# A recommendation tower on one core: weights in paced pieces, another chunk with the batch on the partitions, and gathers without a rest

## The chip, the cores and the metric

The kernel runs on one core of one Trainium2 chip. Times are device microseconds (us) of one execution. The figure that counts is the median of the runs.

## The reference

512 rows (the batch) look up one row of 64 numbers in each of 32 tables. For each of the 496 pairs of fields i < j, the reference takes p (field i) and q (field j), and a 64x64 matrix of that pair, and sums over both sides. The 496 sums of a batch row go through a small tower.

```python
e = jnp.stack([tbl_0[ids[:, 0]], ..., tbl_31[ids[:, 31]]], axis=1)      # 512 x 32 x 64
rows, cols = np.triu_indices(32, k=1)
p, q = e[:, rows, :], e[:, cols, :]
pij = jnp.einsum('bpe,dpe,bpd->bp', p, kernel, q)                        # 512 x 496
z = pij @ W.T + b                                                        # 512 x 256
h = jnp.concatenate([z, dense_ctx], axis=1)
h = jnp.maximum(h @ W_top1 + b_top1, 0.0)
h = jnp.maximum(h @ W_top2 + b_top2, 0.0)
y = h @ W_top3
```

## The kernel before, in words

**Chunks.** Two fields make a chunk, so there are 16 chunks of 128 numbers a batch row, and x_sb holds them with the batch of 512 along the free side. Chunks 0 to 3 (small tables) are picked by matmuls with one-hot matrices (pick_rows): VectorE makes three of four one-hots (L651), ScalarE the fourth. These picks fill the first 43 us. Chunks 4 to 15 are gathered from the tables by indirect DMAs on GpSimd (L339), 8 a chunk (2 fields by 4 tiles of 128 batch rows), 96 in all; gather k belongs to chunk 4 + k // 8. TensorE turns a gathered chunk (L393), and ScalarE copies it to x_sb and own_sb (L585, L589). This pair of steps is called "fill c" here: on TensorE it waits for all gathers up to number 8(c - 3) - 1 (fill 9: gather 47; fill 10: gather 55; fill 11: gather 63).

**Gathers.** A gather waits until the gather two before it has landed (FLIGHT = 2). Behind each gather stands a memset of 380 columns of a buffer that nobody reads (L346), the rest. GpSimd thus issues a gather, rests, and issues the next.

**Pair weights.** kern is loaded into k_sb in 16 slices of 8 blocks. Slices 0 and 1 come in 4 loads of 256 KB (L304), slice 0 right behind the tables of the one-hot fields, slice 1 once fill 0 is done. The other 14 slices come in 8 pieces of 64 KB each (L315), 112 pieces; piece p waits on the SP queue until gather 8 + p * 80 // 112 has landed. The upper half of k_sb is lent to the tables of the picks until fill 3 (L312).

**Units.** The work of TensorE is a fixed list. A group (g0 to g91) is the products of four field pairs with one chunk c (L439, L440; four of them, marked within, pair the fields of four chunks, L443 to L448), so it needs chunk c. VectorE multiplies its result with x_sb (L673), and later a reduce (L460, two for every four groups, called a reduce pair) sums over the 64 rows. A side unit (S0 to S31) does the same work for one quarter of the batch, for a chunk of FAR against the four chunks of NEAR (4 to 7), with the batch on the partitions: two matmuls (L414, L416), one multiply on VectorE with the gathered rows themselves (L660), and 16 sums on ScalarE (L570). A chunk of FAR has four side units, and thereby four groups fewer. t_ps has 3 buffers, so TensorE is at most three units ahead of VectorE; side_prod has 3, so VectorE is at most three side units ahead of ScalarE. There are 92 groups and 32 side units, with the blocks of k_sb in the order of the list.

**Order.** plan() puts fill c min(LEAD, (c - 1) // 2) groups before the first group that needs chunk c, and side unit m behind group SIDE_AT[m]. The order around the change is

```
fill 8 | g19 S2 g20 g21 R S3
fill 9 | g22 g23 g24 S4 g25 R g26 S5
fill 10| g27 g28 S6 g29 R g30 g31 S7
fill 11| g32 g33 R S8 g34 g35 S9 g36 g37 R S10 g38 g39
fill 12| ...
```

where R is a reduce pair. Each engine works through its own part of the list in order; ScalarE's copies for a fill stand behind the sums of the side units that come before that fill.

Of the kernel before, what the change touches and what calls it, by code (L numbers as in the profile page):

```python
# [13 lines left out]
P = 128  # L14
BATCH = 512
FIELDS = 32
EMB = 64
# [26 lines left out]


NEAR = [4, 5, 6, 7]
FAR = [0, 1, 8, 9, 10, 11, 12, 13]
SIDE_TILES = 8 * len(FAR)
SIDE_GROUPS = SIDE_TILES // 2
SIDE_UNITS = BT * len(FAR)  # L50


def is_side(c, a):
    return c in FAR and a in NEAR or c in NEAR and a in FAR


def side_tile(k, s, n):

    return 4 * (8 * (k % 2) + 4 * s + n) + k // 2
# [6 lines left out]
side_tiles = {side_tile(k, s, n): [(2 * c + s, 2 * near), (2 * c + s, 2 * near + 1)]  # L66
              for k, c in enumerate(FAR) for s in range(2) for n, near in enumerate(NEAR)}
GROUP = [(None, False, [side_tiles[2 * g], side_tiles[2 * g + 1]]) for g in range(SIDE_GROUPS)]
# [8 lines left out]
NT = 2 * len(GROUP)  # L77
WITHIN = [g for g in range(GROUPS) if MAIN[g][1]]
FIRST_GROUP = [min(g for g in range(GROUPS) if MAIN[g][0] == c) if c else 0 for c in range(CHUNKS)]
LEAD = 5  # L80

SIDE_AT = [15 + 71 * m // (SIDE_UNITS - 1) for m in range(SIDE_UNITS)]
SIDE = [(c, t) for c in FAR for t in range(BT)]


def plan():

    steps, chunks, side = [], 0, 0  # L90
    for g in range(GROUPS):
        while chunks < CHUNKS and (chunks < max(2, ONE_HOTS) or g >= FIRST_GROUP[chunks] - min(LEAD, (chunks - 1) // 2)):
            steps.append(("fill", chunks))
            chunks += 1
        steps.append(("group", g))
        while side < SIDE_UNITS and SIDE_AT[side] <= g:
            steps.append(("side", side))
# [13 lines left out]
for kind, n in UNITS:  # L111
    if kind == "side":
        c, t = SIDE[n]
        if t == 0:
            SIDE_BLOCK_OF[c] = len(BLOCK)
            BLOCK += [tuple((side_tile(FAR.index(c), s, k), (0, 1), 2 * c + s) for s in range(2)) for k in range(len(NEAR))]
        continue
    _, within, tiles = MAIN[n]
    g = SIDE_GROUPS + n
# [7 lines left out]
KS = 8  # L127
SLICES = BLOCKS // KS
# [13 lines left out]
ROWS_RING = 4  # L142
FLIGHT = 2
REST = 380
WARM = 2
PIECES = 8
PIECES_FROM, GATHERS_AHEAD = 2, 8
GATHERS = 2 * BT * (CHUNKS - ONE_HOTS)
HALF = BATCH // 2

# [10 lines left out]
def gathered_slot(n):  # L161

    return n if n < len(NEAR) else len(NEAR) + (n - len(NEAR)) % (G_RING - len(NEAR))


def build(nc, ids, ids_t, iota, pick, tables, kern, w_pairs, b_int, ctx_rows, w_ctx_rows, w1, b1, w2, b2, w3, ident, selector, out):
    steps = STEPS
    with ExitStack() as ctx:
        def sb(name, shape, dt=F32):
            return ctx.enter_context(nc.sbuf_tensor(name, shape, dt))  # L170

        def sem(name):
            return ctx.enter_context(nc.semaphore(name))
# [11 lines left out]
        k_sb = sb("k_sb", [P, BLOCKS, P])  # L185
# [28 lines left out]
        y_sb = sb("y_sb", [P, P])  # L214
        rest_sb = sb("rest_sb", [P, REST])
        zeros = sb("zeros", [P, BATCH])
# [31 lines left out]
        k_in = [sem(f"k_in{s}") for s in range(SLICES)]  # L248
# [7 lines left out]
        filled = sem("filled")  # L256
# [18 lines left out]
        rested = sem("rested")  # L275
# [11 lines left out]
        @block.sync  # L287
        def _(sp):
            sp.dma_start(ids_sb[:], ids.bitcast(U32).rearrange("(t p) f -> p t f", p=P)).then_inc(ids_in, 16)
            sp.dma_start(ident_sb[:], ident).then_inc(ident_in, 16)  # L290
            for f, field in enumerate(FIRST_FIELDS):
                if f == 4:
                    sp.wait_ge(one_hot_ready, OH_RING * 3 // 4)
                per = PICK[f][0]
                table = tables[field].rearrange("(p r) e -> p (r e)", r=per)
                for rows in (slice(0, DMA_ROWS), slice(DMA_ROWS, V_ROWS)):
                    sp.dma_start(table_sb[rows, f, 0:per].rearrange("p r e -> p (r e)"), table[rows]).then_inc(picks_in[f], 16)
            sp.dma_start(sel_sb[:], selector).then_inc(sel_in, 16)
            for s in range(PIECES_FROM):
                if s == 1:  # L300
                    sp.wait_ge(filled, 1)
                for half in range(2):
                    n = (2 * s + half) * KS * P
                    sp.dma_start(k_sb[half * EMB:(half + 1) * EMB, KS * s:KS * (s + 1), :].rearrange("p g m -> p (g m)"),  # L304
                                 kern[:, n:n + KS * P]).then_inc(k_in[s], 16)

            pieces = [(s, e) for s in range(PIECES_FROM, SLICES) for e in range(0, P, P // PIECES)]
            for p, (s, e) in enumerate(pieces):
                k = GATHERS_AHEAD + p * (GATHERS - 2 * GATHERS_AHEAD) // len(pieces)
                sp.wait_ge(rows_in[k % ROWS_RING], 16 * (k // ROWS_RING + 1))  # L310
                if s == SLICES // 2 and e == 0:
                    sp.wait_ge(filled, ONE_HOTS)  # L312
                half, low = e // EMB, e % EMB
                n = (2 * s + half) * KS * P
                sp.dma_start(k_sb[e:e + P // PIECES, KS * s:KS * (s + 1), :].rearrange("p g m -> p (g m)"),  # L315
                             kern[low:low + P // PIECES, n:n + KS * P]).then_inc(k_in[s], 16)
            for r in range(ROWS_RING):
                sp.wait_ge(rows_in[r], 16 * (GATHERS // ROWS_RING))
            for dst, src in LATE:
                sp.dma_start(dst, src).then_inc(late_in, 16)  # L320
            sp.wait_ge(y_kept, 1)
            sp.dma_start(out.rearrange("(t n) a -> t (n a)", t=BT), y_sb[::32, :]).then_inc(stored, 16)
            sp.wait_ge(stored, 16)

        @block.gpsimd
        def _(pool):
            pool.memset(w3_wide[:], 0.0).then_inc(w3_cleared, 1)
            pool.wait_ge(ids_in, 16)
            for n in range(CHUNKS - ONE_HOTS):
                if n >= G_RING:  # L330
                    pool.wait_ge(filled, n - (G_RING - len(NEAR)) + ONE_HOTS + 1)
                for f in range(2):
                    field = FIELD[2 * (n + ONE_HOTS) + f]
                    for t in range(BT):
                        k = (2 * n + f) * BT + t
                        landed = k - FLIGHT
                        if landed >= 0:
                            pool.wait_ge(rows_in[landed % ROWS_RING], 16 * (landed // ROWS_RING + 1))
                        pool.indirect_dma_start(  # L339
                            gathered[:, gathered_slot(n), t, f * EMB:(f + 1) * EMB], None, tables[field],  # L340
                            bass.IndirectOffsetOnAxis(ap=ids_sb[:, t, field:field + 1], axis=0),
                        ).then_inc(rows_in[k % ROWS_RING], 16)

                        if k:
                            pool.wait_ge(rested, k)
                        pool.memset(rest_sb[:], 0.0).then_inc(rested, 1)  # L346

        @block.tensor
        def _(pe):
            def warm_up():  # L350

                pe.wait_ge(zeros_ready, 1)
                for _ in range(WARM):
                    pe.matmul(sum_ps[:], zeros[:, 0:P], zeros[:], start=True, stop=True)
# [41 lines left out]
            def weights_in(k, blocks):  # L396

                for s in range(SLICES):
                    if k <= s * KS < k + blocks:
                        pe.wait_ge(k_in[s], 16 * (2 if s < PIECES_FROM else PIECES))  # L400

            def side_products(m):

                c, quarter = SIDE[m]
                u = UNITS.index(("side", m))
                k = SIDE_BLOCK_OF[c]
                if quarter == 0:
                    weights_in(k, len(NEAR))
                    pe.wait_ge(x_ready, 2 * (c + 1))
                pe.wait_ge(prod_ready, u - T_RING + 1)  # L410
                t = t_ps[:, u % T_RING]
                cols = slice(quarter * P, (quarter + 1) * P)
                low, high = slice(0, EMB), slice(EMB, P)
                pe.matmul(t[:, 0, :], x_sb[low, c, cols], k_sb[low, k:k + len(NEAR), :].rearrange("p g m -> p (g m)"),  # L414
                          start=True, stop=True)
                pe.matmul(t[:, 1, :], x_sb[high, c, cols], k_sb[high, k:k + len(NEAR), :].rearrange("p g m -> p (g m)"),  # L416
                          start=True, stop=True).then_inc(t_ready, 1)
# [329 lines left out]
```

## Time and profile before

| | us |
|---|---|
| median of 3 runs | 259.27 |
| lowest, highest | 256.65, 260.71 |
| the profiled execution, its time | 258.45 |
| its span | 256.6 |

The span is the stretch that the profile covers; 1.85 us of the execution's time lie around it. In the rows below, a PE row is TensorE's matmuls, PEld its weight loads, DVE VectorE, ACT ScalarE, POOL GpSimd, SPq the queue of SyncE. PE's busy time is modelled and holds short waits inside a run of matmuls; the idle times in brackets are the longer ones.

### The profile page before, as it was taken

The page shows a single profiled execution, that of the slowest core. Times are in us where ns is not written, and L with a number is a line of the kernel's source. Part 1 is how long each engine was busy: PE and PEld are TensorE (multiplying, and loading weights), DVE is VectorE, ACT ScalarE, POOL GpSimd, SP SyncE. Part 2 cuts the span into 40 slices and gives each one's busy share as a digit, 9 for nine tenths or more (in the row PEclk, how much of TensorE's full clock was granted, in tenths as well). Part 3 has the DMA queues.
Part 4 walks back from the last instruction along what each step waited for, and adds up shares of the span by engine and source line. Part 5 has one row for each costly group of instructions (what it writes and reads, how often), then busy time and mean ns, then how long its engine had stood idle before and what let it go on. Part 6 is the DMA issues. An engine that isn't in the chain of part 4 may idle for free.

```text
span 256.6 us, 4466 instructions
## 1 busy us (share of the span) xinstructions
PE 236.2 (92%) x1254; PEld 91.6 (36%) x1254; DVE 183.5 (72%) x205; ACT 174.1 (68%) x1110; POOL 136.9 (53%) x197
## 2 busy tenths in 40 slices
PE   7778789999999397949999999999999999999996
PEld 3433445233332132322243332333333233333474
DVE  2999995867778175845797878988888798860130
ACT  3867777032169908973989989998999969841121
POOL 5766988888888888888888878300000000000000
PEclk9799999999999779988999999999999999999999
DMA  6294232333333233333332321370000000000000
GB/s 163 67 278 117 69 82 61 75 85 88 76 82 82 74 89 77 74 82 76 84 83 72 83 70 25 78 251 3 1 1 3 1 0 3 1 0 0 3 0 0
DMA packets 11035, 16.43 MB, mean 64 GB/s; under 512 B 5166, under 2 KB 5810, under 8 KB 11010
## 3 DMA queue, kind: packets, MB, share of 16 engines
q1 hardware_dynamic: 7768, 12.97, 18.0%
q0 software_dynamic: 3072, 3.15, 6.6%
q8 instruction: 10, 0.16, 0.3%
q14 instruction: 15, 0.12, 0.2%
q10 hardware_dynamic: 170, 0.03, 0.1%
HBM read 16.13 MB, written 0.00 MB: 63 GB/s over the span
## 4 chain that ended last, share of the span: by engine, by line
PE 55%; POOL 26%; DMA 14%; issue 4%; ACT 0%
PE t_ps L439 22%; POOL gathered L339 18%; DMA gathered<-in_tbl,ids_sb 13%; PE sum_ps L460 12%; PE t_ps L414 9%; POOL rest_sb L346 8%; PE t_ps L505 3%; PE tp_ps L467 1%; PE t_ps L514 1%; PE t_ps L467 1%; PE tp_ps L393 1%; PE t_ps L443 1%; DMA ids_sb<-in_ids 1%; PE t_ps L447 1%; PE tp_ps L514 1%
## 5 line engine op out<-in xcount | busy, mean ns | idle before, releaser
L570 ACT ACTIVATE side_prod<-side_prod 128x64 f32<-128x64 f32 x512 | 122.6, 241 | 25.6 <-DVE side_prod L660 21.4
L673 DVE TENSOR_TENSOR prod<-t_ps,x_sb 128x1024 f32<-128x1024 f32 x88 | 104.2, 1216 | 30.2 <-PE t_ps L440 25.7
L339 POOL DMA_INDIRECT gathered<-in_tbl,ids_sb x96 | 94.7, 986 | 25.4 <-issue 13.6
L570 ACT ACTIVATION_READ_ACCUMULATOR side_prod<-side_prod 128x1 f32 x512 | 95.9, 187 | 0.0
L439 PE MATMUL t_ps<-x_sb,k_sb 64*128 64x512 f32 x176 | 92.1, 635 | 0.2
L440 PE MATMUL t_ps<-x_sb,k_sb 64*128 64x512 f32 x176 | 92.2, 635 | 0.0
L439 PEld LDWEIGHTS t_ps<-x_sb,k_sb 64*128 64x128 f32 x176 | 31.0, 193 | 47.5 <-issue 30.8
L460 PE MATMUL sum_ps<-prod,sel_sb 128*32 128x512 f32 x368 | 44.3, 598 | 0.0
L660 DVE TENSOR_TENSOR side_prod<-t_ps,gathered 128x1024 f32<-128x1024 f32 x32 | 38.9, 1216 | 7.1 <-PE t_ps L416 5.4
L346 POOL MEMSET rest_sb<- 128x380 f32 x96 | 42.1, 438 | 0.1
L416 PE MATMUL t_ps<-k_sb,x_sb 64*128 64x512 f32 x64 | 33.9, 610 | 0.0
L414 PE MATMUL t_ps<-k_sb,x_sb 64*128 64x512 f32 x64 | 33.9, 610 | 0.0
L440 PEld LDWEIGHTS t_ps<-x_sb,k_sb 64*128 64x128 f32 x176 | 31.0, 193 | 0.0
L651 DVE TENSOR_SCALAR pair_sums<-ids_bc,iota_sb 125x512 bf16<-125x512 f16 x57 | 24.3, 488 | 1.7 <-issue 1.2
L460 PEld LDWEIGHTS sum_ps<-prod,sel_sb 128*32 128x32 f32 x368 | 9.6, 109 | 31.9 <-issue 25.4
L585 ACT COPY x_sb<-tp_ps 128x512 f32<-128x512 f32 x14 | 8.1, 578 | 18.2 <-issue 11.3
L381 PE MATMUL tp_ps<-pair_sums,k_sb 125*64 125x512 bf16 x72 | 15.9, 410 | 4.5 <-DVE pair_sums L651 1.7
L414 PEld LDWEIGHTS t_ps<-k_sb,x_sb 64*128 64x128 f32 x64 | 10.9, 186 | 19.8 <-issue 11.1
L393 PE MATMUL tp_ps<-ident_sb,gathered 128*128 128x128 f32 x48 | 8.3, 299 | 10.2 <-DMA gathered<-in_tbl,ids_sb 9.7
L381 PE MATMUL sum_ps<-pair_sums,k_sb 125*64 125x512 bf16 x76 | 14.6, 382 | 1.7 <-DVE pair_sums L651 1.0
L553 ACT ACTIVATE distance<-ids_bc,iota_sb 125x512 f16<-125x512 f16 x17 | 12.1, 713 | 1.8 <-PE tp_ps L381 1.6
L393 PEld LDWEIGHTS tp_ps<-ident_sb,gathered 128*128 128x128 f32 x48 | 5.3, 147 | 19.6 <-issue 18.5
(66 smaller groups left out, 171.3 us busy)
## 6 DMA issues: line engine op xcount, KB each, us to landing
k_sb<-in_kern SPq DMA_DIRECT2D x112, 64.0 KB
gathered<-in_tbl,ids_sb POOLq DMA_INDIRECT x96
k_sb<-in_tbl SPq DMA_DIRECT2D x5, 280.0 KB
k_sb<-in_kern SPq DMA_DIRECT2D x4, 256.0 KB
w_sb<-in_w SPq DMA_DIRECT2D x2, 512.0 KB, 5.2
k_sb<-in_tbl SPq DMA_DIRECT2D x3, 224.0 KB
w_pairs_sb<-in_w_pairs SPq DMA_DIRECT2D x1, 512.0 KB, 3.6
ctx_sb<-in_ctx_rows SPq DMA_DIRECT2D x1, 192.0 KB, 6.0
```

The source lines that it names most:

```text
L339: pool.indirect_dma_start(gathered[:, gathered_slot(n), t, f * EMB:(f + 1) * EMB], None, tables[field], bass.IndirectOffsetOnAxis(ap=ids_s ...
L346: pool.memset(rest_sb[:], 0.0).then_inc(rested, 1)
L381: mm = pe.matmul(bank[half:half + EMB, :], part[:, f, r, :], one_hot[:, n % OH_RING, :], start=(r == 0 and part is high_sb), stop=(r == PI ...
L414: pe.matmul(t[:, 0, :], x_sb[low, c, cols], k_sb[low, k:k + len(NEAR), :].rearrange("p g m -> p (g m)"), start=True, stop=True)
L416: pe.matmul(t[:, 1, :], x_sb[high, c, cols], k_sb[high, k:k + len(NEAR), :].rearrange("p g m -> p (g m)"), start=True, stop=True).then_inc ...
L439: pe.matmul(t[:, 0, :], k_sb[low, k, :], x_sb[low, a, :], start=True, stop=True)
L440: pe.matmul(t[:, 1, :], k_sb[high, k, :], x_sb[high, a, :], start=True, stop=True).then_inc(t_ready, 1)
L460: mm = pe.matmul(sum_ps[32 * j:32 * j + 32, :], sel_sb[:, 30 - 2 * k:62 - 2 * k], prod[:, (t // 2) % PROD_RING, t % 2, :], start=(k == 0), ...
L570: one = act.activation(part, part, ACT.Copy, accum_out=side_sums[:, t, 16 * k + n:16 * k + n + 1])
L651: dve.tensor_scalar(one_hot[:, n % OH_RING, :], ids_bc[:, f, :], iota_sb[:, PICK[f][1] + r:PICK[f][1] + r + 1], None, ALU.is_equal).then_i ...
L660: dve.tensor_tensor(side_prod[:, g % SIDE_RING].rearrange("p s (c n) -> p s c n", c=len(NEAR)), t_ps[:, u % T_RING].rearrange("p s (c n) - ...
L673: dve.tensor_tensor(prod[:, g % PROD_RING], t_ps[:, u % T_RING], q, ALU.mult).then_inc(prod_ready, 1)
```

## The change

The pair weights of all 16 slices come in paced pieces (128 of them; piece p waits for gather 8 + p * 80 // 128, so slice s is asked for by gather 5s + 12 at the latest). The 4 loads of 256 KB and their wait are gone. FAR has chunk 14 in place of chunk 8. Chunk 8 thereby has 8 groups and no side units, chunk 14 has 10 groups and 4 side units; the totals stay. LEAD is 4 in place of 5, and SIDE_AT ends at 85 in place of 86. The first 16 gathers have no rest.

```diff
-FAR = [0, 1, 8, 9, 10, 11, 12, 13]
+FAR = [0, 1, 9, 10, 11, 12, 13, 14]
-LEAD = 5
+LEAD = 4
-SIDE_AT = [15 + 71 * m // (SIDE_UNITS - 1) for m in range(SIDE_UNITS)]
+SIDE_AT = [15 + 70 * m // (SIDE_UNITS - 1) for m in range(SIDE_UNITS)]
+NO_REST = 16
-PIECES_FROM, GATHERS_AHEAD = 2, 8
+GATHERS_AHEAD = 8
-            for s in range(PIECES_FROM):
-                if s == 1:
-                    sp.wait_ge(filled, 1)
-                for half in range(2):
-                    n = (2 * s + half) * KS * P
-                    sp.dma_start(k_sb[half * EMB:(half + 1) * EMB, KS * s:KS * (s + 1), :].rearrange("p g m -> p (g m)"),
-                                 kern[:, n:n + KS * P]).then_inc(k_in[s], 16)
-
-            pieces = [(s, e) for s in range(PIECES_FROM, SLICES) for e in range(0, P, P // PIECES)]
+            pieces = [(s, e) for s in range(SLICES) for e in range(0, P, P // PIECES)]
-                        if k:
-                            pool.wait_ge(rested, k)
-                        pool.memset(rest_sb[:], 0.0).then_inc(rested, 1)
+                        if k >= NO_REST:
+                            if k > NO_REST:
+                                pool.wait_ge(rested, k - NO_REST)
+                            pool.memset(rest_sb[:], 0.0).then_inc(rested, 1)
-                        pe.wait_ge(k_in[s], 16 * (2 if s < PIECES_FROM else PIECES))
+                        pe.wait_ge(k_in[s], 16 * PIECES)
```

The list after the change, from the same place on:

```
fill 8 | g19 S2 g20 g21 R S3 g22 g23 g24 S4 g25 R
fill 9 | g26 S5 g27 g28 S6 g29 R g30 S7
fill 10| g31 g32 g33 R S8 g34 g35 S9 g36
fill 11| g37 R S10 g38 g39 S11 g40 g41 R g42 S12 g43 g44 S13
fill 12| ...
```

Here g22 to g29 need chunk 8, g30 to g34 chunk 9, g35 to g40 chunk 10, g41 on chunk 11. The order up to fill 8 is unchanged.

## Rows read from the trace of the kernel before

**Rows 1.** The page, part 1: busy us (share of the span) and instructions of each engine.

```profile
PE 236.2 (92%) x1254; PEld 91.6 (36%) x1254; DVE 183.5 (72%) x205; ACT 174.1 (68%) x1110; POOL 136.9 (53%) x197
```

**Rows 2.** Waits, longest first: engine, line, awaited, us in total, times, longest.

```profile
PE tp_ps L393 <- DMA gathered<-in_tbl,ids_sb: 9.7, 3, 4.5
...
POOL gathered L339 <- DMA gathered<-in_tbl,ids_sb: 9.6, 15, 1.7
```

**Rows 3.** Timeline of PE around the three waits: start us, us, line, count, idle before.

```profile
82.63 0.59 PE L414 MATMUL t_ps<-k_sb,x_sb 64*128 64x512 f32 x1
...
87.76 1.09 PE L393 MATMUL tp_ps<-ident_sb,gathered 128*128 128x128 f32 x4 [4.53 <-DMA gathered<-in_tbl,ids_sb]
...
101.16 0.63 PE L393 MATMUL tp_ps<-ident_sb,gathered 128*128 128x128 f32 x4 [1.82 <-DMA gathered<-in_tbl,ids_sb]
```

**Rows 4.** Busy by stretch: PE, PEld, DVE, ACT, POOL, then granted clock, DMA share, GB/s.

```profile
83.20:87.80 4.60, 0.07 (x3) 0.07 (x2) 1.22 (x1) 4.60 (x41) 4.10 (x7) 0.86 0.33 83
87.80:93.20 5.40, 5.40 (x14) 2.51 (x16) 1.81 (x2) 2.52 (x15) 4.74 (x8) 0.50 0.31 76
...
99.30:101.20 1.90, 0.08 (x3) 0.07 (x2) 1.58 (x2) 1.20 (x11) 1.45 (x3) 1.00 0.23 56
101.20:110.00 8.80, 8.80 (x48) 3.30 (x48) 6.23 (x6) 8.29 (x63) 7.84 (x12) 1.00 0.35 85
110.00:113.40 3.40, 0.06 (x3) 0.04 (x1) 1.87 (x2) 1.84 (x17) 2.93 (x6) 1.00 0.31 72
113.40:117.50 4.10, 4.10 (x12) 1.56 (x12) 1.23 (x1) 3.48 (x23) 3.60 (x6) 0.58 0.32 76
```

**Rows 5.** The chain that ended last, in order of time: start us, us, what.

```profile
12.62 5.77 DMA gathered<-in_tbl,ids_sb
18.64 4.69 DMA gathered<-in_tbl,ids_sb
...
97.99 3.04 DMA gathered<-in_tbl,ids_sb
...
110.59 2.56 DMA gathered<-in_tbl,ids_sb
113.39 0.73 PE tp_ps L393 x4
...
117.58 1.85 PE sum_ps L460 x16
119.43 0.62 PE t_ps L414
120.06 0.42 PE t_ps L414
...
227.15 0.59 PE tp_ps L423 x4
```

**Rows 6.** Timeline of PE: the end of group g36.

```profile
123.48 0.59 PE L439 MATMUL t_ps<-x_sb,k_sb 64*128 64x512 f32 x1
```

**Rows 7.** Timeline of POOL: gathers 9, 10, 16, 47, and a rest between.

```profile
23.59 0.95 POOL L339 DMA_INDIRECT gathered<-in_tbl,ids_sb  x1 [0.88 <-DMA gathered<-in_tbl,ids_sb]
24.54 0.52 POOL L346 MEMSET rest_sb<- 128x380 f32 x1
25.23 1.07 POOL L339 DMA_INDIRECT gathered<-in_tbl,ids_sb  x1 [0.16 <-issue]
...
36.00 1.07 POOL L339 DMA_INDIRECT gathered<-in_tbl,ids_sb  x1 [0.16 <-issue]
...
85.14 0.95 POOL L339 DMA_INDIRECT gathered<-in_tbl,ids_sb  x1 [0.17 <-issue]
```

**Rows 8.** Busy by stretch, as rows 4, while tables and slices 0 and 1 load.

```profile
16.00:18.00 2.00, 0.87 (x8) 0.59 (x10) 2.00 (x6) 0.55 (x1) 0.92 (x2) 1.00 1.05 284
...
22.00:24.00 2.00, 1.76 (x12) 0.60 (x8) 1.97 (x4) 1.94 (x4) 1.12 (x3) 1.00 0.14 29
```

**Rows 9.** Timeline of SP: the four large loads and the first pieces.

```profile
14.90 4.26 SPq L304 DMA_DIRECT2D k_sb<-in_kern  x4
24.33 35.82 SPq L315 DMA_DIRECT2D k_sb<-in_kern  x31
```

**Rows 10.** Timeline of ACT: first and last of the 32 instructions of S3, then fill 9.

```profile
85.36 0.24 ACT L570 ACTIVATE side_prod<-side_prod 128x64 f32<-128x64 f32 x1
...
89.08 0.19 ACT L570 ACTIVATION_READ_ACCUMULATOR side_prod<-side_prod 128x1 f32 x1
89.17 0.57 ACT L585 COPY x_sb<-tp_ps 128x512 f32<-128x512 f32 x1
89.77 0.58 ACT L589 COPY own_sb<-tp_ps 64x512 f32<-64x512 f32 x1
```

## The prediction

> **What bounds the kernel now.** I read the page's busy shares first. TensorE is busy for 92% of the span, the others for at most 72% [rows 1]. A busy share does not say what stands in the other 8%, so the list of waits comes next: TensorE's longest wait for data is for gathers, 9.7 us in three waits of up to 4.5 us, in front of a turn [rows 2]. The timeline places them: fill 9 starts at 87.76 after 4.5 us idle, fill 10 at 101.16 after 1.8 us, fill 11 at 113.39 [rows 3, 5], where the gap is 3.3 us [rows 4]. The view by stretch shows what follows: behind the first wait the granted clock is 0.50 for 5.4 us and behind the third 0.58 for 4.1 us, which is TensorE's 1.2 GHz level; behind the 1.8 us wait it stays 1.00, 2.4 GHz [rows 4]. So three gathers (47, 55, 63) decide when TensorE goes on, and after fill 11 the chain that ended last stays on TensorE [rows 5]. From there on no gather is waited for. What is saved before fill 11 reaches the end; what is saved on gathers after it does not.
>
> **Part 1: chunk 14 for chunk 8, LEAD 4, SIDE_AT.** The number of products is the same. What moves is work that needs nothing newer than chunk 8: it now stands in front of fills 9, 10 and 11. The prices: a unit is two steps of 0.42 to 0.43 us, 0.86 us, a reduce pair takes 1.85 us, a turn at full clock about 0.6 us [rows 3, 5].
>
> TensorE reaches the wait of fill 9 at 83.2 now (its last side matmul starts at 82.63 and lasts 0.59) [rows 3]. After the change five units and a reduce pair stand there first: 83.2 + 5 x 0.86 + 1.85 + 0.2 for changes between kinds = 89.6. Gather 47 started at 85.14 [rows 7] and had landed by 87.6 (fill 9 started at 87.76). So no wait, and no slow clock.
>
> Fill 10 then comes after the turn, 8 units and a reduce pair: 89.6 + 0.6 + 6.9 + 1.85 = 99.0; with 0.6 for VectorE, which must keep up through three buffers, 99.6. Gather 55 landed at 97.99 + 3.04 = 101.0 [rows 5]. With gathers where they are, 1.4 us of wait are left and fill 10 starts at 101.2.
>
> Fill 11 comes again after a turn, 8 units and a reduce pair, 9.7 us: 110.9. Gather 63 landed at 110.59 + 2.56 = 113.15 [rows 5]: fill 11 starts at 113.4 as now, after 2.5 us idle, and ends at 114.0.
>
> What has been gained there: g0 to g36 and S0 to S9 are done. Before, that state (its fill 11 included) is reached at 123.48 + 0.5 = 124.0 [rows 6]. So 10.0 us, if gathers stay where they are and 2.5 us of idle do not lower the clock. Between 1.8 us (clock kept) and 3.3 us (clock lowered) the rows leave this open; if it falls, up to 1.7 us go back (four steps and a turn took 4.1 us at 0.58 in place of some 2.4) [rows 4]. The rest, from 124.0 to the end at 256.6, is 132.6 us of the same work.
>
> **Part 2: no rest for 16 gathers.** A rest takes 0.43 to 0.52 us, with 0.16 before the next gather; gathers 9 to 16 start 12.4 us apart in seven steps, 1.77 each (23.59 to 36.00) [rows 7]. Without it the limit is the landing of the gather two before. The undisturbed landing is 2.56 us after the start, and the next gather follows 0.26 us behind a landing (12.62 + 5.77 = 18.39 to 18.64) [rows 5], so the least step is (2.56 + 0.26)/2 = 1.41 us. Seven steps give back 7 x 0.36 = 2.5 us. Gathers 2 to 8 wait for landings already and gain little by this.
>
> **Part 3: no large loads.** Landings of 5.8 and 4.7 us are those of gathers 5 and 7, beside tables and slices 0 and 1; the DMA engines move 284 GB/s then, and 29 GB/s from 22 on [rows 5, 8]. The four loads, 1.0 MB, are issued from 14.90 on [rows 9]. At about 250 GB/s they hold the engines for 4 us. Without them gathers 6 to 9 come up to 4 us earlier; the lower bound is 0, if the tables alone delay them. I take 2.5, since the tables are queued first.
>
> The bill comes later. 128 pieces instead of 112 go beside the same 80 gathers, 1.6 each instead of 1.4. GpSimd waits for landings 15 times now, 9.6 us [rows 2]; the landing of gather 55, 3.04, is what two pieces close together cost. Up to gather 63 I take 1 us back, and another 1 us because gathers 16 on, now earlier, run beside the one-hots, where the gather instruction takes 1.07 instead of 0.95 us [rows 7]. Sum for gathers 47 to 63: 2.5 + 2.5 - 2 = 3 us earlier. Bounds: 1 us later (nothing gained, pieces cost) to 5 us earlier.
>
> The Trainium skill has a rule against this part. Its page "SBUF — State Buffer" (section "SBUF: two separate sides", with the box on the "DVE blocks DMA" trap) says that VectorE in a two-port mode, which tensor_scalar can take, shuts GpSimd out and starves it of descriptor writes. The trace agrees in sign, 1.07 beside 0.95 us, but not with a full block. By the rule the first 16 gathers gain nothing from the missing rest, which would leave rival A below.
>
> Are slices 0 and 1 in time? Slice 0 needs gather 12, slice 1 gather 17. Gather 16 starts at 36.00 now, so gather 12 has landed by 33 and slice 0 is in by 36; the first group runs at 43.7, and slice 1 is needed at about 53, in by 43. Covered even with no gain. The later slices are asked for up to 10 gathers later than now and needed tens of us after that.
>
> **Sum.** With gathers 3 us earlier, gather 55 lands at 98.0: no wait at fill 10 (99.6). Fill 11 is reached at 109.3, plus 0.4 for ScalarE's copy of chunk 10 (below): 109.7. Gather 63 lands at 110.2, fill 11 starts at 110.4 and ends at 111.0, at full clock. 111.0 + 132.6 = 243.6. Add 1.0 for ScalarE: **span 244.6, 12.0 us less**. The profiled time would be 258.45 - 12.0 = 246.4. The median shown is 0.8 above the profiled one: 259.27 - 12.0 = 247.3. I take **247.5**.
>
> **ScalarE.** The sums of a side unit take 3.8 us (85.36 to 89.17), a fill's copies 1.15 [rows 10]. Now ScalarE has gaps (busy 2.5 of the 5.4 us from 87.8) [rows 4]; after the change it has none: S3 ends at 89.2, S4 93.1, fill 9 94.3, S5 98.2, S6 102.1, S7 106.0, copies of fill 10 107.1. The first group of chunk 10, g35, would be reached at 106.7. So LEAD 4 costs 0.4 us there. Then come 24 side units (91.2), five fills (5.8) and three windows (0.6 each): 205.9. TensorE turns the side sums at 227.15 now [rows 5], 13 us earlier then, 214: ScalarE is done 8 us before. Counted the same way from fill to fill, its copies are 2 to 4 us ahead of the first groups. I take 1 us in all, at most 4.
>
> **Rivals.**
> A. Gathers come no earlier (the landing or the shared port holds them). Gain 10.0 - 1.0 for ScalarE, less up to 1.7 for the clock: 250.3 to 252.0, say 250.5. For it: gathers 2 to 8 wait for landings anyway, and the instruction is longer beside one-hots. Against it: gathers 10 to 16 wait for nothing but the rest [rows 7]. The page above would give this case.
> B. ScalarE becomes the bound: with LEAD 4 each of fills 10 to 15 waits about 1 us, and the rest costs 5 to 6 us instead of 1: gain about 7, 252.5. For it: it has no gap from 81 us on. Against it: the 8 us by which its sum stays short of TensorE's.
> C. Not faster: more pieces raise the landing. Before nothing is lost until the step exceeds a gather's own 1.55 us, that is a landing of 2.84. To eat the whole gain, gather 63 must land at 123.4, 10 us later: over 55 gathers 0.19 us a step, a mean landing of about 3.4 to 3.5 us. Such landings occur (3.04 for gather 55), but as exceptions. At a mean of 3.6, 262.
>
> **Chances.** Forecast (gathers 1.5 to 5 us earlier, 245 to 249) 0.53; even better, 244 to 245, 0.04; A (249 to 252) 0.25; B (252 to 255) 0.10; C (255 and more) 0.08. The range 244 to 252.5 holds 0.83 and leaves out C and most of B. A measurement of this kernel tells 2% from no change, 5.2 us: faster means below 254.1, chance 0.89; within 2% 0.08; slower 0.03.
>
> **What would show it.** Fill 9 starts without idle at about 89.6; fill 10 at 99.6; fill 11 by 110.4; granted clock 1.00 from 40 us on; gather 16 starts by 32, gather 47 by 82; GpSimd's waits for landings below 13 us in total; ScalarE busy without gaps from 81 us. Wrong: a new wait of TensorE for x_sb at the first group of a chunk (B), a step of the gathers above 1.8 (C), or first groups that wait for k_in.

## The result, and the profile after

| | before | after |
|---|---|---|
| median, us | 259.05 (4 runs) | 247.51 (4 runs) |
| lowest, highest | 256.65, 260.71 | 246.80, 248.09 |
| profiled execution, its time | 258.45 | 247.30 |
| its span | 256.6 | 245.5 |

The ratio is 0.9583, with a 95% interval of 0.9511 to 0.9656: 4.2% faster. This and all later ratios are of fast executions alone, where one that is more than 1.5% above the fastest of its kernel counts as slow. The code is some lines shorter, so L339 of before is L333 in the trace of after, L393 is L388, L439 L434, L460 L455, L585 L580, L589 L584. The kernels of the experiments have line numbers of their own, a few lines off.

The page of after, part 1 (busy us, share of the span, instructions), answers [rows 1]; the waits (us in total, times, longest) answer [rows 2]:

```profile
PE 232.3 (95%) x1254; PEld 89.8 (37%) x1254; DVE 177.0 (72%) x205; ACT 173.5 (71%) x1110; POOL 128.6 (52%) x181
```

```profile
POOL gathered L333 <- DMA gathered<-in_tbl,ids_sb: 16.5, 24, 2.1
...
PE tp_ps L388 <- DMA gathered<-in_tbl,ids_sb: 4.2, 3, 2.3
```

TensorE's waits for gathers fell from 9.7 to 4.2 us, 0.7 of it at fill 7. Its timeline (start us, us, line, idle before) at the first group and at fills 9, 10 and 11, against [rows 3, 5]:

```profile
40.49 0.69 PE L434 MATMUL t_ps<-x_sb,k_sb 64*128 64x512 f32 x1
...
87.03 0.66 PE L388 MATMUL tp_ps<-ident_sb,gathered 128*128 128x128 f32 x4
...
98.42 0.63 PE L388 MATMUL tp_ps<-ident_sb,gathered 128*128 128x128 f32 x4 [1.19 <-DMA gathered<-in_tbl,ids_sb]
...
110.66 0.63 PE L388 MATMUL tp_ps<-ident_sb,gathered 128*128 128x128 f32 x4 [2.34 <-DMA gathered<-in_tbl,ids_sb]
```

Fill 9 waits for nothing, as forecast. Fills 10 and 11 start at 98.42 and 110.66, where 99.6 and 110.4 were forecast, but both still wait. Two things in these rows were not forecast. The first group starts at 40.49 us instead of 43.71 (before: L439, first row of its kind), and the clock falls again behind fill 11. The view by stretch (columns as in [rows 4]):

```profile
108.30:110.70 2.40, 0.06 (x3) 0.07 (x2) 2.23 (x2) 2.40 (x22) 1.88 (x3) 1.00 0.41 103
110.70:115.70 5.00, 5.00 (x24) 1.25 (x24) 1.22 (x1) 4.15 (x28) 4.22 (x7) 0.66 0.34 80
```

The reduce pair behind fill 11 takes 3.1 us at this clock instead of 1.85. Gathers 16 and 63 on GpSimd, against [rows 5, 7] (36.00 and 110.59 there):

```profile
32.82 0.94 POOL L333 DMA_INDIRECT gathered<-in_tbl,ids_sb  x1 [0.30 <-issue]
...
108.09 0.95 POOL L333 DMA_INDIRECT gathered<-in_tbl,ids_sb  x1 [0.16 <-issue]
```

Gather 63 starts 2.5 us earlier; 3 us was forecast.

The experiments were to test these theories. G: only the time of the last gather waited for (63) and the work done before it decide. M: the rests on GpSimd hold up VectorE's one-hots. L, the rival of M: the large loads did. The executions of one kernel lie 1 to 5 us apart, a trace shows only one of them, and the intervals of the ratios are 1.1 to 1.7% wide. So small differences of the time show nothing unless the intervals are apart. Where a trace is compared with another, it is one execution against one.

### The profile page after: what moved, and what is told of

The parts are those of the page before. It is cut to its first block, busy times and chain, and to the rows that moved or that the text cites. A ratio compares the mean times of both kernels' runs of the same rounds, so it can differ in the third digit from the quotient of the medians.

```text
span 245.5 us, 4460 instructions
## 1 busy us (share of the span) xinstructions
PE 232.3 (95%) x1254; PEld 89.8 (37%) x1254; DVE 177.0 (72%) x205; ACT 173.5 (71%) x1110; POOL 128.6 (52%) x181
## 4 chain that ended last, share of the span: by engine, by line
PE 54%; DMA 22%; POOL 18%; issue 4%; ACT 0%
DMA gathered<-in_tbl,ids_sb 21%; PE t_ps L434 20%; POOL gathered L333 13%; PE sum_ps L455 12%; PE t_ps L409 8%; POOL rest_sb L341 5%; PE t_ps L500 3%; PE tp_ps L462 2%; PE t_ps L509 1%; PE t_ps L462 1%; PE tp_ps L388 1%; DMA ids_sb<-in_ids 1%; PE t_ps L438 1%; PE t_ps L442 1%; PE sum_ps L509 1%
## 5 line engine op out<-in xcount | busy, mean ns | idle before, releaser
L333 POOL DMA_INDIRECT gathered<-in_tbl,ids_sb x96 | 93.7, 976 | 32.5 <-DMA gathered<-in_tbl,ids_sb 16.5
L435 PE MATMUL t_ps<-x_sb,k_sb 64*128 64x512 f32 x176 | 88.7, 614 | 0.0
L434 PE MATMUL t_ps<-x_sb,k_sb 64*128 64x512 f32 x176 | 88.6, 613 | 0.1
L434 PEld LDWEIGHTS t_ps<-x_sb,k_sb 64*128 64x128 f32 x176 | 29.7, 185 | 45.2 <-issue 29.4
L455 PE MATMUL sum_ps<-prod,sel_sb 128*32 128x512 f32 x368 | 45.5, 613 | 0.0
L341 POOL MEMSET rest_sb<- 128x380 f32 x80 | 34.7, 433 | 0.0
L435 PEld LDWEIGHTS t_ps<-x_sb,k_sb 64*128 64x128 f32 x176 | 29.7, 185 | 0.0
L646 DVE TENSOR_SCALAR pair_sums<-ids_bc,iota_sb 125x512 bf16<-125x512 f16 x57 | 18.7, 385 | 4.2 <-ACT ids_bc L532 2.0
L455 PEld LDWEIGHTS sum_ps<-prod,sel_sb 128*32 128x32 f32 x368 | 9.8, 111 | 32.6 <-issue 28.0
L580 ACT COPY x_sb<-tp_ps 128x512 f32<-128x512 f32 x14 | 8.1, 581 | 16.4 <-PE tp_ps L388 11.0
L376 PE MATMUL tp_ps<-pair_sums,k_sb 125*64 125x512 bf16 x72 | 14.9, 410 | 3.1 <-DVE k_sb L625 1.7
L388 PE MATMUL tp_ps<-ident_sb,gathered 128*128 128x128 f32 x48 | 7.8, 284 | 4.5 <-DMA gathered<-in_tbl,ids_sb 4.2
L551 ACT ACTIVATE pair_sums<-distance 125x512 bf16<-125x512 f16 x17 | 10.7, 630 | 0.5
```

The costliest lines, as they stand in the source:

```text
L333: pool.indirect_dma_start(gathered[:, gathered_slot(n), t, f * EMB:(f + 1) * EMB], None, tables[field], bass.IndirectOffsetOnAxis(ap=ids_s ...
L376: mm = pe.matmul(bank[half:half + EMB, :], part[:, f, r, :], one_hot[:, n % OH_RING, :], start=(r == 0 and part is high_sb), stop=(r == PI ...
L434: pe.matmul(t[:, 0, :], k_sb[low, k, :], x_sb[low, a, :], start=True, stop=True)
L435: pe.matmul(t[:, 1, :], k_sb[high, k, :], x_sb[high, a, :], start=True, stop=True).then_inc(t_ready, 1)
L455: mm = pe.matmul(sum_ps[32 * j:32 * j + 32, :], sel_sb[:, 30 - 2 * k:62 - 2 * k], prod[:, (t // 2) % PROD_RING, t % 2, :], start=(k == 0), ...
L646: dve.tensor_scalar(one_hot[:, n % OH_RING, :], ids_bc[:, f, :], iota_sb[:, PICK[f][1] + r:PICK[f][1] + r + 1], None, ALU.is_equal).then_i ...
```

## The experiments

**One part alone: no rest behind 16 gathers** (e1_norest_alone), on the kernel before.

```diff
-                        if k:
-                            pool.wait_ge(rested, k)
-                        pool.memset(rest_sb[:], 0.0).then_inc(rested, 1)
+                        if k >= NO_REST:
+                            if k > NO_REST:
+                                pool.wait_ge(rested, k - NO_REST)
+                            pool.memset(rest_sb[:], 0.0).then_inc(rested, 1)
```

> The kernel before with one part: no rest behind the first 16 gathers. The trace after shows one-hots of VectorE at a mean of 385 ns against 488 before and the first group at 40.5 us against 43.7. If the rests on GpSimd hold the one-hots up (theory M), the one-hots have a mean near 385 to 400 here too, and the first group starts near 40.5. If it was the 1 MB of large loads beside them (theory L), it stays at 43.7. For the end, theory G (three gathers bound this order, the speed of the picks is worth nothing): only the shift of gathers 47 and 63 counts, 1 to 2.5 us, so 256.5 to 258 us. If the picks counted, the gain would be 3 us or more beside that of the gathers, under 254.

Ratio 0.9899 (0.9842 to 0.9956), 1.0%; the medians of all runs are 257.31 and 258.32. The groups of instructions of VectorE from 5 to 45 us (count, busy us, mean ns) in the kernel before and in this one, then the first group, gathers 16 and 63, and the turns of fills 9, 10 and 11:

```profile
L651 DVE TENSOR_SCALAR pair_sums<-ids_bc,iota_sb 125x512 bf16<-125x512 f16 x57 | 24.3, 488 | 1.7 <-issue 1.2 <-PE sum_ps L381 0.2
```

```profile
L653 DVE TENSOR_SCALAR pair_sums<-ids_bc,iota_sb 125x512 bf16<-125x512 f16 x57 | 19.4, 398 | 3.7 <-ACT ids_bc L539 1.8 <-PE sum_ps L383 1.1 <-PE tp_ps L383 0.5
```

```profile
41.10 0.69 PE L441 MATMUL t_ps<-x_sb,k_sb 64*128 64x512 f32 x1
```

```profile
33.28 0.94 POOL L340 DMA_INDIRECT gathered<-in_tbl,ids_sb  x1 [0.31 <-DMA gathered<-in_tbl,ids_sb]
...
107.56 0.95 POOL L340 DMA_INDIRECT gathered<-in_tbl,ids_sb  x1 [0.17 <-issue]
```

```profile
85.34 1.08 PE L395 MATMUL tp_ps<-ident_sb,gathered 128*128 128x128 f32 x4 [4.86 <-DMA gathered<-in_tbl,ids_sb]
...
98.13 0.63 PE L395 MATMUL tp_ps<-ident_sb,gathered 128*128 128x128 f32 x4 [1.95 <-DMA gathered<-in_tbl,ids_sb]
...
110.09 0.63 PE L395 MATMUL tp_ps<-ident_sb,gathered 128*128 128x128 f32 x4 [1.37 <-DMA gathered<-in_tbl,ids_sb]
```

Theory M holds: with this edit alone the one-hots take 398 ns and TensorE's groups start 2.6 us earlier. Gather 16 comes 2.7 us earlier, as the prediction worked out (2.5), and 63 comes 3.0 earlier. By the ratio the end gains 1.0%, about 2.6 us (its interval is 1.1 to 4.1 us), which fits the gathers' shift. The profiled execution gains more: it is the fastest of ten (253.37; two more lie below 254.5 and the rest at 256.7 to 258.3), and its span is 5.2 us shorter than that of before. Its trace shows from what. Fill 9 still waits 4.9 us, so the earlier picks are lost there. Fill 11 starts 3.3 us earlier, with the gathers. The other 1.9 us come from the clock. Here it fell behind fill 10 (0.70 from 98.1 to 102.0), and that delay only shortened the wait at fill 11; behind fill 11 it stayed at 1.00, where before it was 0.58 for 4.1 us. So theory G holds for the gathers, and the clock behind the last wait is a second term of about 2 us. Whether the same term explains the spread of the ten is not shown, since only one was profiled.

**One part alone: all weights in paced pieces** (e2_pieces_alone). The changed kernel with FAR, LEAD, SIDE_AT of before and NO_REST = 0.

> The kernel before with one part: all 16 slices of the weights in paced pieces, with rests behind all gathers. Theory L: the first group starts near 40.5 us, one-hots near 385 ns. Theory M: 43.7 and 488 as before. The landing of gathers 5 and 6 falls from 5.8 and 6.1 us to about 4, so gather 9 starts 2 to 3 us earlier; 128 pieces give 1 us back by gather 63. Theory G: 1 to 2 us faster than before, 257 to 258.5.

Ratio 0.9923 (0.9869 to 0.9976).

```profile
L646 DVE TENSOR_SCALAR pair_sums<-ids_bc,iota_sb 125x512 bf16<-125x512 f16 x57 | 23.9, 480 | 1.9 <-ACT ids_bc L532 1.4 <-PE sum_ps L376 0.2
```

```profile
22.13 1.06 POOL L333 DMA_INDIRECT gathered<-in_tbl,ids_sb  x1 [0.17 <-issue]
...
111.14 0.95 POOL L333 DMA_INDIRECT gathered<-in_tbl,ids_sb  x1 [0.17 <-issue]
```

Theory L falls: one-hots at 480 ns, first group at 43.69. Gather 9 (first row) starts at 22.13, 1.5 us earlier than before, but gather 63 at 111.14, 0.55 later. The profiled execution, 258.69 us, is at the upper end of this kernel's runs (254.2 to 259.1); the ratio says 0.8% faster, and this trace does not show from what.

**One part alone: the order** (e3_order_alone).

```diff
-FAR = [0, 1, 8, 9, 10, 11, 12, 13]
+FAR = [0, 1, 9, 10, 11, 12, 13, 14]
-LEAD = 5
+LEAD = 4
-SIDE_AT = [15 + 71 * m // (SIDE_UNITS - 1) for m in range(SIDE_UNITS)]
+SIDE_AT = [15 + 70 * m // (SIDE_UNITS - 1) for m in range(SIDE_UNITS)]
```

> The kernel before with one part: chunk 14 in place of chunk 8, LEAD 4, SIDE_AT 70. Theory G: the prediction's own sum with gathers where they are, 10.0 us less 1.0 for ScalarE and up to 1.7 for the clock: 249.5 to 252. Fill 9 without idle, fill 10 about 1.4 us, fill 11 about 2.5 us idle. A rival that gives the gathers most of the gain: under 4 us, above 255.

Median 249.77, ratio 0.9677 (0.9623 to 0.9730): 8.3 us. Fills 9, 10 and 11:

```profile
88.73 0.66 PE L393 MATMUL tp_ps<-ident_sb,gathered 128*128 128x128 f32 x4
...
100.90 0.63 PE L393 MATMUL tp_ps<-ident_sb,gathered 128*128 128x128 f32 x4 [1.96 <-DMA gathered<-in_tbl,ids_sb]
...
113.20 0.63 PE L393 MATMUL tp_ps<-ident_sb,gathered 128*128 128x128 f32 x4 [2.40 <-DMA gathered<-in_tbl,ids_sb]
```

Fill 9 without a wait, fills 10 and 11 within 0.3 us of the forecast 101.2 and 113.4. Behind the wait of 2.4 us the clock is 0.64 for 4.8 us. Against the kernel before, the ratios of e3 and of the full change are 0.9677 and 0.9583: by these ratios the order carries about three quarters of the gain (3.2 of 4.2%). Their intervals overlap, so the last quarter is not shown by the times.

**The rests put back** (e4_order_pieces): the changed kernel with NO_REST = 0.

> The changed kernel with the rests behind the first 16 gathers put back. Theory G: the end moves by what gather 63 loses, 1.5 to 2.5 us, so 249 to 250, and the slower picks (theory M: first group at 43.7 again) cost nothing beside that; fill 11 waits less than in the changed kernel (0 to 1 us instead of 2.3) and the clock stays up. If the picks counted: 3 us and more slower, above 250.5.

Median 249.97, ratio 0.9657 (0.9582 to 0.9732), beside e3's 0.9677: adding the pieces to the order changes nothing that can be measured. In its trace gather 16 starts at 35.46, gather 63 at 111.79 and fill 11 at 114.47 after 2.46 us idle. Gather 63 is 1.4 us later than in e3, with 16 pieces more. The expectation that fill 11 would wait at most 1 us was wrong: against the changed kernel the gathers lost as much (3.7 us) as TensorE's first group did (3.6). So this run cannot tell the cost of the gathers from that of the picks. Its profiled execution is also the slowest of its four, 251.08.

**The large loads put back** (e5_order_norest): order and missing rests, 4 loads of 256 KB and 112 pieces.

> The changed kernel with the 4 large loads of slices 0 and 1 back in place of 16 paced pieces (112 pieces over the same gathers). By the prediction the large loads delay gathers 6 to 9, so gather 63 would come 1.5 us later and the time be 248.5 to 249. By the runs of the single parts (gather 63 at 107.6 us with no rest alone and 112 pieces, at 108.1 in the changed kernel) the pieces give back by gather 63 what they gain by gather 9: gather 63 at 107.3 to 107.8, the time 246.5 to 247.5, the same within 0.3%.

Median 248.15 (247.4 to 248.5), ratio 0.9611 (0.9552 to 0.9671), not told apart from the changed kernel. Gather 63 at 108.97, 0.9 later than in the changed kernel; with e1 against the changed kernel it was 0.5 earlier and with e3 against e4 1.4 earlier. The pieces move gather 63 by no more than the scatter, to either side.

**LEAD 5** (e6_lead5).

```diff
-LEAD = 4
+LEAD = 5
```

> The changed kernel with LEAD 5 in place of 4, all else the same. The turns stand one group earlier in the list, so fill 11 is reached 0.9 us earlier and waits 0.9 us more for the same gather, with fewer groups done: 248 to 249, 1 to 1.5 us slower. If ScalarE's copies were late with LEAD 4 (rival B of the prediction), LEAD 5 would be faster instead: 245 to 246.5.

Ratio 0.9613 (0.9526 to 0.9700), median 248.76. Fill 10 waits 2.46 us, fill 11 3.33 (1.19 and 2.34 with LEAD 4), in an execution, the slowest of four, whose gather 63 was itself 2.2 us later. The direction is that of theory G; the ratio does not tell the two apart.

**No rest behind 64 gathers** (e7_norest64): NO_REST = 64.

> The changed kernel with no rest behind the first 64 gathers instead of 16. Theory G with steps at half the landing: landings of 2.6 to 3.1 us give steps of 1.43 to 1.68 against 1.62 now between gathers 16 and 47 and 1.56 up to 63; gather 63 starts 2 to 5 us earlier, fills 10 and 11 wait at most 1 us, the clock stays up: 243 to 245.5. Rival: the rest is what keeps the landings short; without it they grow to 3.1 and more, steps stay at 1.6 or rise, 247 to 249.

Median 248.86, ratio 0.9655 (0.9595 to 0.9715), not faster than the changed kernel. The profiled execution is the fastest of six, 245.57. Its waits:

```profile
POOL gathered L333 <- DMA gathered<-in_tbl,ids_sb: 35.1, 38, 1.9
```

Gather 16 at 32.43, gather 47 at 82.92: 1.63 us a step against 1.62 with rests, and gather 63 at 107.62. The rival holds: what GpSimd no longer rests it waits for landings, 35.1 us instead of 16.5. Beyond gather 16 the rest costs nothing.

**Two memsets as a rest** (e8_double_rest16): two memsets of 380 columns behind each of the first 16 gathers.

> The changed kernel with two memsets of 380 columns behind each of the first 16 gathers, where it has none and the kernel before one. Theory M, each memset holds up one-hots: mean of the one-hots 385 ns with none, 474 to 488 with one, 540 to 600 with two; first group at 45 to 47 us against 40.5 and 43.7. If instead any GpSimd instruction that is on slows them alike, gathers too, the mean stays under 500. The gathers themselves come later: gather 16 near 38 to 40, time 252 to 256.

One run of 252.7 us. One-hots at a mean of 497 ns, first group at 44.91, gather 16 at 38.99. The mean is below what was expected of theory M, since fewer gathers and so only 1.7 times as many memsets fall beside the picks; it lies even below the 500 that the expectation named as the sign of the other reading, that any GpSimd instruction slows the one-hots alike. The mean does not by itself tell memsets from other GpSimd work; the single one-hots and the run e11 below do. VectorE's timeline in the kernel before, four one-hots around the memset at 26.29 (0.47 us) that follows the gather at 25.23 [rows 7]:

```profile
25.39 0.34 DVE L651 TENSOR_SCALAR pair_sums<-ids_bc,iota_sb 125x512 bf16<-125x512 f16 x1
25.65 0.76 DVE L651 TENSOR_SCALAR pair_sums<-ids_bc,iota_sb 125x512 bf16<-125x512 f16 x1
26.33 0.58 DVE L651 TENSOR_SCALAR pair_sums<-ids_bc,iota_sb 125x512 bf16<-125x512 f16 x1
26.83 0.33 DVE L651 TENSOR_SCALAR pair_sums<-ids_bc,iota_sb 125x512 bf16<-125x512 f16 x1
```

A one-hot takes 0.34 us and starts 0.26 behind the one before. Two are longer. The one of 0.76 lies beside the end of the gather and the start of the memset, the one of 0.58 over the memset. Their followers start 0.68 and 0.50 behind them: 0.66 us lost for one gather and its rest. In the changed kernel, beside a gather without a rest (29.92 to 31.00), only one of the row is longer, and by 0.15:

```profile
30.36 0.35 DVE L646 TENSOR_SCALAR pair_sums<-ids_bc,iota_sb 125x512 bf16<-125x512 f16 x1
30.62 0.49 DVE L646 TENSOR_SCALAR pair_sums<-ids_bc,iota_sb 125x512 bf16<-125x512 f16 x1
31.04 0.34 DVE L646 TENSOR_SCALAR pair_sums<-ids_bc,iota_sb 125x512 bf16<-125x512 f16 x1
```

The longest one-hot beside a gather without a rest is 0.55 us here; one of 0.74 stands at gather 16, the first that is followed by a rest again. So both the gather and the memset take time from VectorE, and the memset takes the larger part. An estimate for one memset: VectorE is busy with the one-hots for 24.3 us in the kernel before, with 18 memsets beside them, and for 17.5 in e11 with none, which makes 0.4 us each.

**One step further** (e9_chunk15): more work in front of fill 11.

```diff
-FAR = [0, 1, 9, 10, 11, 12, 13, 14]
+FAR = [0, 1, 10, 11, 12, 13, 14, 15]
-SIDE_AT = [15 + 70 * m // (SIDE_UNITS - 1) for m in range(SIDE_UNITS)]
+SIDE_AT = [15 + 18 * m // 7 if m < 8 else 35 + 50 * (m - 8) // 23 for m in range(SIDE_UNITS)]
```

> The changed kernel one step further: FAR is 0, 1, 10 to 15 (chunk 15 in place of chunk 9), and the side units stand at SIDE_AT = 15 to 33 for the first 8, then 35 to 85, since S8 now needs fill 10. Fill 10 stands behind 43 units in place of 39, fill 11 behind 52 in place of 47. Theory G: TensorE reaches fill 10 at 102.6 us and fill 11 at about 113, both behind their gathers (98.2 and 110.5): the waits of 1.2 and 2.3 us and 1.7 us of slow clock go, 5.2 us: 242 to 243.5 us. Rival: ScalarE or VectorE becomes the bound, since the side units stand closer at the end: 245 to 248.

Median 249.7, ratio 0.9663 (0.9601 to 0.9725). Fills 9 to 11 no longer wait, at 87.08, 102.59 and 120.02. But the first side unit of chunk 10, S8, stands one unit behind fill 10. TensorE, then ScalarE in front of it:

```profile
108.08 1.19 PE L409 MATMUL t_ps<-k_sb,x_sb 64*128 64x512 f32 x1 [3.77 <-issue]
```

```profile
103.11 0.26 ACT L565 ACTIVATE side_prod<-side_prod 128x64 f32<-128x64 f32 x1 [0.83 <-DVE side_prod L655]
106.94 0.56 ACT L580 COPY x_sb<-tp_ps 128x512 f32<-128x512 f32 x1
107.40 0.58 ACT L584 COPY own_sb<-tp_ps 64x512 f32<-64x512 f32 x1
```

Fill 10 was turned at 102.6; its copies had to wait for the 16 sums of S7 until 106.9. TensorE idled 3.8 us and ran 4.4 us at a clock of 0.50. The forecast of 242 to 243.5 was missed by 6 us, and the time lies above its rival's 245 to 248 too. That rival had ScalarE as the bound, but neither named this place.

**The same with rests** (e10_chunk15_rests): e9 with NO_REST = 0.

> As e9_chunk15, with the rests behind the first 16 gathers put back. Where no gather is waited for, the picks must count: the first group starts 3 us later (43.7 against 40.5) and so does everything, 3 us slower than e9_chunk15, 245 to 246.5. Rival: the rests cost only through the gathers; then, with no gather waited for, nothing: within 1 us of e9_chunk15.

Median 251.17, ratio 0.9720 (0.9668 to 0.9772), 1.5 us over e9 with overlapping intervals. The traces: first group 43.86 against 40.03, fill 10 105.13 against 102.59, neither of them behind a wait for a gather; spans 250.3 and 247.8. So in these two executions, where TensorE waits for no gather from fill 9 on, 2.5 us of the picks' 3.8 come through; e9 had lost 1.2 to gathers at two earlier fills.

**No rest beside any pick** (e11_chunk15_rest24): e9 with NO_REST = 24.

> As e9_chunk15, with no rest behind the first 24 gathers instead of 16, so that no memset runs beside any pick. With 24, the last four or five memsets beside one-hots go: first group 0.3 to 1 us earlier, the time 0 to 1 us less, 241.5 to 243. If memsets are not what holds VectorE up, no difference.

Median 249.45, ratio 0.9688 (0.9620 to 0.9755): no difference. The one-hots:

```profile
L646 DVE TENSOR_SCALAR pair_sums<-ids_bc,iota_sb 125x512 bf16<-125x512 f16 x57 | 17.5, 362 | 6.1 <-ACT ids_bc L532 2.1 <-PE sum_ps L376 2.1 <-PE tp_ps L376 1.2
```

Their mean falls to 362 ns (e9: 397) although 18 gathers start beside them: this fits theory M, since gathers alone add little to the 340 ns of an undisturbed one-hot. But the first group is no earlier (40.91, e9: 40.03). VectorE now waits 6.1 us between one-hots, most of it for ScalarE and TensorE, so it is no longer the bound of the picks.

**LEAD 3** (e12_lead3).

```diff
-LEAD = 4
+LEAD = 3
-SIDE_AT = [15 + 70 * m // (SIDE_UNITS - 1) for m in range(SIDE_UNITS)]
+SIDE_AT = [16 + 70 * m // (SIDE_UNITS - 1) for m in range(SIDE_UNITS)]
```

> The changed kernel with LEAD 3 and all side units one group later (SIDE_AT from 16 to 86). ScalarE's own list keeps its order, each turn stands one unit later on TensorE, and a reduce pair moves in front of fill 11. Theory G: fill 10 is reached 0.9 us later and waits 0.3 us instead of 1.2; fill 11 is reached near 110 us and waits under 1 us instead of 2.3, so the clock is not lowered (1.7 us); more is done by then, 0.9 + 1.9 us: 243.5 to 245. Rival: ScalarE's copies are now too late, since the first group stands one closer to its fill while the copy waits behind side sums (as in e9_chunk15, where TensorE idled 3.8 us behind fill 10): new waits of 1 to 3 us at several fills, 247 to 250.

Median 249.83 (6 runs; the profiled one, 251.76, is the slowest), ratio 0.9687 (0.9636 to 0.9737); the rival holds. No fill from 4 on waits for a gather in its trace. These rows of TensorE's timeline stand in their place, and they are all its idle times of over 0.3 us between 60 and 215 us:

```profile
79.90 0.66 PE L434 MATMUL t_ps<-x_sb,k_sb 64*128 64x512 f32 x1 [0.73 <-ACT own_sb L584]
106.65 1.19 PE L434 MATMUL t_ps<-x_sb,k_sb 64*128 64x512 f32 x1 [2.28 <-ACT own_sb L584]
...
137.28 1.11 PE L434 MATMUL t_ps<-x_sb,k_sb 64*128 64x512 f32 x1 [2.24 <-ACT own_sb L584]
...
192.51 0.67 PE L434 MATMUL t_ps<-x_sb,k_sb 64*128 64x512 f32 x1 [1.56 <-ACT own_sb L584]
```

6.8 us of waits for ScalarE's copies, with slow clock behind two of them (0.51 and 0.54), replace 3.5 us of waits for gathers. The changed kernel sits between two bounds: later turns run into ScalarE, earlier ones into the gathers. None of the variants was faster by its ratio; e5 and e6 are not told apart from it.

## Why the prediction was right, and where it was not

247.5 was forecast and 247.51 measured. The mechanism holds, but that close a hit is luck. For the profiled execution 246.4 was forecast and 247.30 measured, 0.9 us more (span 244.6 and 245.5): fill 11 ended 0.2 later, the clock cost 1.7 that the sum did not have, and the 1.0 for ScalarE was not needed. The allowance from the profiled time to the median was 0.8, plus 0.2 by rounding up; it turned out as 0.2 and took those 0.9 back.

**The bound.** Three gathers decided: shown. The order alone, which moves only work, gives 8.3 us, and the prediction's sum for gathers that stay (10.0, less 1.0 for ScalarE and up to 1.7 for the clock, so 7.3 to 9.0) holds it.

**No rest.** Forecast 2.5 us by gather 16, measured 2.7 (e1 against before) and 2.6 (the changed kernel against e4). The marks named for the changed kernel, gather 16 by 32 us and 47 by 82, were missed by 0.8 and 1.1 us.

**No large loads.** This term failed. It gave 2.5 us by gather 9 and took 2 back by gather 63, for pieces and one-hots. Measured alone (e2): 1.5 by gather 9, and by gather 63 nothing or less (0.55 us later); e4 and e5 agree within their scatter. The sum of both parts, 3, still met the 2.5 of the changed kernel, since the term of the rests kept its 3.0 to gather 63 alone.

**The picks.** They were not in the sum at all. The prediction saw gathers longer beside one-hots (1.07 instead of 0.95 us) and did not ask the reverse. The rests cost VectorE about 100 ns a one-hot over 57 one-hots, and the first group 3.2 us. The section that it had cited, of the Trainium skill, page "SBUF — State Buffer", section "SBUF: two separate sides", has both directions: of a VectorE instruction in a two-port mode and a GpSimd instruction, whichever starts first keeps the shared pair of ports for the whole instruction, and the other waits. The rows agree in direction, with 0.76 and 0.58 us for one-hots of 0.34. They do not show a wait as long as the GpSimd instruction: beside a gather of 0.95 us without a rest no one-hot takes more than 0.55. No row shows which mode the one-hots ran in. That the memsets hold up the one-hots is shown by e1 and e11; that they do so by the shared ports is the page's reading and was not tested here. I had read the rule for the gathers only.

**Fills 10 and 11.** TensorE came to fill 10 at 97.2, not 99.6, since the picks were early, and waited 1.2 us where none was forecast, then 2.3 where 0.7 was. The start of fill 11 is the gather's, 110.66 against 110.4. This is why the picks' 3.2 us are not in the result: they became waiting. Behind the second wait the clock fell (0.66 for 5.0 us), 1.7 us that the forecast had given as not paid. After fill 11, at 111.2, 132.6 us of the old trace plus 1.7 more make 245.5, the measured span.

**ScalarE.** The 1 us for it was not paid: no wait of TensorE for a copy shows after 60 us, and ScalarE had gaps of 1 to 3 us (at 106, 118 and 128), where none were forecast. But the bound was as near as feared in rival B: one group less of lead (e12, with the side units one group later), or a side unit close behind its fill (e9), and it decides.

**Rivals.** A is what e4 shows (no rest gained, 249.97, forecast 250.5). C did not occur: GpSimd's waits for landings rose from 9.6 to 16.5 us, over the 13 named as the limit, but its steps stayed at 1.6. C's own arithmetic was off: by the prediction's formula (a step is half the sum of the landing and 0.26) a gather 63 that is 10 us later asks for a mean landing of about 3.3 us, not 3.4 to 3.5, and a mean of 3.6 puts it some 17 us later, so to more than the 262 stated.

## What to carry to other kernels

When an engine waits for a paced stream, first count what work needs nothing from it and stands behind the wait; moving that was worth about three quarters of the gain here. Making the stream faster seems to have given the rest, which is within the noise of the times. A gain upstream of such a wait turns into waiting, and idle time costs again when TensorE's clock falls behind it. And before moving a turn, ask in which order the copying engine gets to it: the lead between producer and user is counted in that engine's queue, not in TensorE's.

## What the runs showed of the hardware that I had not expected

A memset on GpSimd into a buffer that nobody reads slows VectorE's 16-bit tensor_scalar: mean 474 to 488 ns with rests (457 in e3), 381 to 398 without rests behind the first 16 gathers, 361 to 362 with none beside the picks.

Whether the clock falls does not go by the length of the last gap alone: it stayed at 1.00 behind gaps of 1.8 to 2.3 us (2.32 at fill 10 of e7) and fell behind 2.21 (e8, 0.66) and 1.95 (e1, 0.70). What decides in between stayed open.

Gathers issued without a rest between them, two in flight, came no faster than with a rest of 0.43 us: 1.63 against 1.62 us a step over 31 gathers (e7 and the changed kernel).
